# Attention and feed-forward layers in one kernel: products ordered by array shape, TensorE's stream written out, the shifted x sent sooner, the norm's tiles on ScalarE

## What is computed

```python
for i in range(DEPTH):                       # DEPTH = 6
    x = attn_layer(shift_tokens(x), Wqkv[i], q_scale[i], k_scale[i], Wo[i]) + x
    x = ffn_layer(shift_tokens(x), ln_g[i], ln_b[i], W1[i], b1[i], W2[i], b2[i]) + x
# shift_tokens: the second half of the features comes from the token before
# attn_layer: 16 heads of 64; q, k = l2norm(...) * scale, rotated; softmax(8 q k^T) over
#   the own window of 32 tokens and the one before; times v; times Wo
# ffn_layer: (x - mean) / sqrt(var + 1e-5) * g + b; a * gelu(gate) @ W2 + b2, hidden size 341
```

## Time and profile before

| | |
|---|---|
| median of three runs | 4655.95 us |
| profiled execution, its span | 4656.79 us, 4655.0 us |
| TensorE: matmuls, weight loads | 4112.3 us (88%), 2362.1 us (51%) |
| VectorE, ScalarE, GpSimd | 3561.9 (77%), 2988.6 (64%), 2212.4 us (48%) |
| mean granted clock of TensorE | 0.935 of full speed |
| stretch of the layers | from about 340 to 3780 us of the span |

### The profile page before, as it was taken

How to read it: one execution, slowest core, us unless ns; L and a number is a source line. 1 busy time by engine, 2 the same in 40 slices (tenths; PEclk the granted TensorE clock), 3 DMA queues, 4 the chain that set the end, 5 groups by cost and what they waited for, 6 DMA issues and landing times. The chain is left out here.

```text
span 4655.0 us, 112822 instructions
## 1 busy us (share of the span) xinstructions
PE 4112.3 (88%) x40172; PEld 2362.1 (51%) x40175; DVE 3561.9 (77%) x8496; ACT 2988.6 (64%) x5496; POOL 2212.4 (48%) x1392
## 2 busy tenths in 40 slices
PE   8969999999999999999999999999999953747635
PEld 5644555555555555555555555555555532635533
DVE  7878888888888888888888888888888846356441
ACT  3427777777777777777777777777777745645302
POOL 0006665665656656566566656656565500140006
PEclk9989999999999999999999999999999975868557
DMA  1013222322223222232222322223222200000202
GB/s 41 1 54 67 62 58 62 80 59 61 60 60 81 63 59 60 58 82 65 59 59 60 76 65 63 57 64 75 64 60 61 58 17 12 1 1 6 82 9 35
DMA packets 187828, 246.44 MB, mean 53 GB/s; under 512 B 88677, under 2 KB 129383, under 8 KB 187367
## 3 DMA queue, kind: packets, MB, share of 16 engines
q1 hardware_dynamic: 182054, 240.47, 22.2%
q0 software_dynamic: 5632, 4.33, 0.7%
HBM read 41.65 MB, written 14.30 MB: 12 GB/s over the span
## 5 line engine op out<-in xcount | busy, mean ns | idle before, releaser
L1234 POOL TENSOR_TENSOR f_rot_a<-f_rot_a,f_norm 128x1024 f32<-128x1024 f32 x384 | 730.4, 1902 | 996.1 <-DVE f_norm L1073 963.6
L1226 POOL TENSOR_TENSOR f_rot_a<-f_rot_a,f_rot_b 128x1024 f32<-128x1024 f32 x384 | 908.5, 2366 | 246.3 <-issue 213.6
L832 PE MATMUL f_bank<-f_w_vo,f_xs_t 128*64 128x512 f32 x3072 | 828.5, 617 | 24.5 <-ACT f_vo L1303 24.5
L1303 ACT ACTIVATE f_vo<-f_bank 128x512 f32<-128x512 f32 x768 | 457.0, 595 | 395.9 <-PE f_bank L832 385.9
L1294 ACT ACTIVATE f_squares<-f_bank 128x512 f32<-128x512 f32 x768 | 456.4, 594 | 295.5 <-PE f_bank L819 215.6
L1052 DVE TENSOR_TENSOR f_rot_a<-f_bank,f_rot 128x512 f32<-128x512 f32 x768 | 525.0, 684 | 83.4 <-DVE f_stat L1101 42.3
L1055 DVE TENSOR_TENSOR f_rot_b<-f_bank,f_rot 128x512 f32<-128x512 f32 x768 | 516.8, 673 | 0.0
L864 PEld LDWEIGHTS f_bank<-f_k_t,f_q_t 128*32 128x32 f32 x12288 | 313.6, 109 | 315.4 <-issue 162.4
L1059 DVE TENSOR_REDUCE f_sums<-f_squares 128x16 f32<-128x1024 f32 x384 | 464.9, 1211 | 1.6
L1315 ACT ACTIVATE f_k_t<-f_bank 64x512 f32<-64x512 f32 x768 | 449.2, 585 | 4.8 <-PE f_bank L854 0.3
L1240 POOL TENSOR_TENSOR f_prob<-f_score,f_stat 128x512 f32<-128x512 f32 x384 | 400.4, 1043 | 98.6 <-DVE f_stat L1105 98.6
(11 more groups left out here) (445 smaller groups left out, 7235.4 us busy)
## 6 DMA issues: line engine op xcount, KB each, us to landing
f_vo_off<-f_vo SPq DMA_DIRECT2D x1152, 128.0 KB, 2.3
f_vo_off<-f_vo SPq DMA_DIRECT2D x384, 64.0 KB, 2.0
f_w_qk<-in_Wqk SPq DMA_DIRECT2D x12, 512.0 KB, 5.9
f_vo_dram<-f_vo_pair SPq DMA_DIRECT2D x48, 128.0 KB, 1.8
f_x_shifted<-s_all SPq DMA_DIRECT2D x48, 128.0 KB
f_x_shifted<-s_all SPq DMA_DIRECT2D x48, 127.0 KB
f_w_vo<-f_vo_dram SPq DMA_DIRECT2D x10, 512.0 KB, 4.0
e_w<-in_e_W SPq DMA_DIRECT2D x2, 2048.0 KB, 12.1
```

The lines of the kernel that those rows point to most:

```text
L832: done = nc.tensor.matmul(bank[V][64 * n:64 * n + 64, :], x, w_vo[:, 4 * g:4 * g + 4, n, :], start=True, stop=True)
L1226: nc.gpsimd.tensor_tensor(rot_a[:, slot, :, :], rot_a[:, slot, :, :], rot_b[:, g, :, :], ALU.add).then_inc(rot_summed, 1)
L1234: nc.gpsimd.tensor_tensor(heads, heads, over(norm[:, 16 * g:16 * g + 16], [128, 16, HEAD_DIM]), ALU.mult).then_inc(qk_normed, 1)
L1303: nc.scalar.activation(vo[:, g, 2 * (t % 2) + j, :], flat(V), ACT.Copy).then_inc((va_copied, vb_copied)[j], 1)
```

## The change

The order of the products in TensorE's body changes so that the value products, the scores and the mix stand in two blocks of four a step; a value product is cut into four parts of 32 columns instead of two of 64. TensorE's loop over passes 3 to 47 is written out; the class `Steady` makes these passes take the loop's branches. The bodies of the other engines are put into an order that goes with it: on VectorE both rotations of k stand together, `total` and `invert` of group 1 always come a step later, `highest` comes after the rotations of q; on ScalarE `exponential` of group 1 always stands ahead of `copy_q`, and the value copies and the other exponential move; on GpSimd `weigh` goes ahead of `scale`. `shift_x` is issued ahead of `shift_values(p, r - 1, 1)` in the third step. The feed-forward norm's four tiles go from VectorE (`normalise`, subtract and multiply) to ScalarE (scale and offset), in two halves in the second step, and VectorE makes the offset, -mean x inverse root, for all four tiles in one small operation.

```diff
@@ -469,6 +469,16 @@
+class Steady(int):
...
+  def __add__(self, n):
+    return Steady(int(self) + n)
...
+  def __sub__(self, n):
+    return Steady(int(self) - n)
...
 def shifted_layers(nc, x_all, ident, ident_bf, dram):
@@ -584,11 +595,11 @@
-      return not isinstance(p, int) or 0 <= p * PASS_TILES + t < LAST * PASS_TILES
+      return not isinstance(p, int) or isinstance(p, Steady) or 0 <= p * PASS_TILES + t < LAST * PASS_TILES
...
-      return not isinstance(p, int) or 0 <= p - back < LAST
+      return not isinstance(p, int) or isinstance(p, Steady) or 0 <= p - back < LAST
@@ -708,6 +719,9 @@
             shift_values(p, r - 1, 0)
+          if r == 2 and (q > 0 or not first):
+            shift_x(p - 1, (q - 1) % PASSES)
+          if r > 0 or q > 0 or not first:
             shift_values(p, r - 1, 1)
@@ -728,8 +742,6 @@
               load_pair(p + 1)
-          if r == 2 and (q > 0 or not first):
-            shift_x(p - 1, (q - 1) % PASSES)
           if q == 0 and r == 2 and not first:
...
               good_for_layer(w_vo_in[g], layer)
@@ -828,8 +840,9 @@
         x = chunk_x(t)[:, 64 * j:64 * j + 64]
-        for n in range(2):
-          done = nc.tensor.matmul(bank[V][64 * n:64 * n + 64, :], x, w_vo[:, 4 * g:4 * g + 4, n, :], start=True, stop=True)
+        for w in range(4):
+          at = 32 * (w % 2)
+          done = nc.tensor.matmul(bank[V][32 * w:32 * w + 32, :], x[:, at:at + 32], w_vo[:, 4 * g:4 * g + 4, w // 2, :], start=True, stop=True)
         return done
       def values_a(p, t, g):
@@ -962,7 +975,6 @@
           if on(r - 1):
-            values_a(p, r - 1, 1)
             turn_q(p, r - 1, 0)
...
             turn_prob(p, r - 2, 0)
@@ -970,7 +982,6 @@
             turn_k(p, r - 1, 0)
-            values_b(p, r - 1, 1)
           if on(r):
...
           if r == 0 and has(p, 0):
@@ -979,8 +990,15 @@
             up_proj(p - 2, 0)
...
           if on(r - 1):
+            values_a(p, r - 1, 1)
             scores(p, r - 1, 0)
+          if on(r - 2):
+            mix(p, r - 2, 0)
+          if on(r - 1):
+            values_b(p, r - 1, 1)
...
             turn_q(p, r - 1, 1)
...
             project_q(p, r, 1)
@@ -997,18 +1015,18 @@
             up_proj(p - 2, 1)
-          if on(r - 2):
-            mix(p, r - 2, 0)
...
           if on(r):
             values_a(p, r, 0)
+          if on(r - 2):
+            mix(p, r - 2, 1)
           if on(r - 1):
...
             values_b(p, r, 0)
-          if on(r - 2):
-            mix(p, r - 2, 1)
...
-      stream(pe, body)
...
+      for p in range(LAST + 3):
+        body(Steady(p) if 3 <= p < LAST else p)
...
     def _(dve):
@@ -1120,18 +1138,15 @@
-      def normalise(p):
+      def offsets(p):
...
         if live(p + 2, 0):
...
         if has(p, 1):
-          dve.wait_ge(f_turned, p)
-        for t in range(PASS_TILES):
-          last = nc.vector.tensor_scalar(f_n[:, 128 * t:128 * t + 128], x_shifted[:, t, :], f_mv[:, t, 0:1], norm[:, 32 + t:33 + t], ALU.subtract, ALU.mult)
-          if t < PASS_TILES - 1:
-            chain.mark(last)
-        last.then_inc(f_normed, 1)
+          dve.wait_ge(f_normed, p + 1)
+        nc.vector.scalar_tensor_tensor(f_offset[:, :], f_mv[:, :, 0], -1.0, norm[:, 32:32 + PASS_TILES], ALU.mult, ALU.mult).then_inc(f_measured, 1)
...
         n = FF[k][1]
@@ -1153,45 +1168,43 @@
             rotate(p, r, 0, 1, 0)
-          if r < 3 and on(r - 2):
-            invert(1)
-          if on(r):
             rotate(p, r, 0, 1, 1)
-          if r == 3 and on(r - 2):
+          if on(r - 2):
             total(p, r - 2, 1)
...
           if r == 1 and has(p, 2):
-            normalise(p - 2)
+            offsets(p - 2)
           if on(r - 3):
...
             length(p, r, 0)
-            rotate(p, r, 1, 1, 0)
           if on(r - 1):
             highest(p, r - 1, 0)
+          if on(r):
+            rotate(p, r, 1, 1, 0)
           if r == 1 and has(p, 3):
...
             rotate(p, r, 1, 1, 1)
+          if on(r - 1):
+            total(p, r - 1, 0)
+            invert(0)
           if on(r):
...
             inverse_lengths(p, r)
-          if on(r - 1):
-            total(p, r - 1, 0)
-            invert(0)
           if r == 3 and has(p, 2):
             hide(p - 2, 1)
-          if on(r - 1):
-            highest(p, r - 1, 1)
           if on(r):
...
             rotate(p, r, 1, 0, 1)
+          if on(r - 1):
+            highest(p, r - 1, 1)
           if r == 0 and has(p, 2) and not on(r):
...
             chain.mark(inverse_roots(32, 32 + PASS_TILES))
@@ -1199,8 +1212,6 @@
             aggregate()
-          if r != 2 and on(r - 1):
-            total(p, r - 1, 1)
         chain.reset()
       stream(dve, body)
@@ -1254,10 +1265,10 @@
             add_up(p, r, 0)
-            scale(p, r, 0)
           if on(r - 1):
...
           if on(r):
+            scale(p, r, 0)
             add_up(p, r, 1)
       stream(pool, body)
@@ -1335,6 +1346,15 @@
+      def normalise(p, half):
+        act.wait_ge(f_measured, p + 1)
+        if half == 0 and has(p, 1):
+          act.wait_ge(f_turned, p)
+        for t in (2 * half, 2 * half + 1):
+          last = nc.scalar.activation(f_n[:, 128 * t:128 * t + 128], x_shifted[:, t, :], ACT.Identity, bias=f_offset[:, t:t + 1], scale=norm[:, 32 + t:33 + t])
+        if half == 1:
+          last.then_inc(f_normed, 1)
...
       def affine(p):
...
         act.wait_ge(f_turned, p + 1)
@@ -1363,37 +1383,39 @@
             shift_in(0, p + 1)
-          if r < 3 and on(r - 2):
+          if on(r - 2):
             exponential(p, r - 2, 1)
           if on(r - 1):
-            copy_values(p, r - 1, 1, 0)
             copy_q(p, r - 1, 0)
-          if r == 3 and on(r - 2):
-            exponential(p, r - 2, 1)
           if on(r - 2):
...
             square(p, r, 0, 0)
+          if r == 1 and has(p, 2):
+            normalise(p - 2, 0)
           if on(r - 1):
...
             seed(p, r - 1, 0)
-            copy_values(p, r - 1, 1, 1)
           if on(r):
             square(p, r, 1, 1)
+          if r == 1 and has(p, 2):
+            normalise(p - 2, 1)
           if r == 0 and has(p, 0):
...
           if on(r - 1):
+            copy_values(p, r - 1, 1, 0)
+            exponential(p, r - 1, 0)
+            seed(p, r - 1, 1)
+            copy_values(p, r - 1, 1, 1)
             copy_q(p, r - 1, 1)
...
             square(p, r, 1, 0)
-          if on(r - 1):
-            exponential(p, r - 1, 0)
-            copy_k(p, r - 1, 1)
-            seed(p, r - 1, 1)
           if on(r - 2):
             copy_prob(p, r - 2, 1)
+          if on(r - 1):
+            copy_k(p, r - 1, 1)
           if on(r):
...
           if r == 0 and has(p, 0):
```

More of the change, by code:

```diff
@@ L533, in shifted_layers @@
         f_mv = sb("f_mv", [128, PASS_TILES, 2])
+        f_offset = sb("f_offset", [128, PASS_TILES])
         f_n = sb("f_n", [128, PASS_TOK])
@@ L575, in shifted_layers @@
         f_gate, gate_in, f_gelu, f_up = sem("f_gate"), sem("gate_in"), sem("f_gelu"), sem("f_up")
-        f_hidden, f_done, x_stored = sem("f_hidden"), sem("f_done"), sem("x_stored")
+        f_hidden, f_done, x_stored, f_measured = sem("f_hidden"), sem("f_done"), sem("x_stored"), sem("f_measured")
         ctx.callback(clear, nc, used)
```

## The result

The changed kernel takes 4727.2 us (median of 4 runs, 4720.9 to 4732.4) against 4655.7 (4 runs): 1.015 times the time before, interval 1.0135 to 1.017. It is 71 us slower where I predicted 20 us faster, and outside my range of 4515 to 4715. The profiled execution took 4724.9, its span is 4723.1.

What follows compares the result with a forecast made beforehand. TensorE's stream was taken as the bound: a pass of 70.7 us less 2.3 (old waits) and 4.7 (shapes), plus 6.6 (new waits), gives 70.3; over 48 passes -20, so 4656 becomes 4636 us, range 4515 to 4715.

Steps and rivals of the forecast that it cites:

- What bounds the kernel: Whole loop: the pass goes at the pace of TensorE's stream; only shortening it or making it wait counts.
- The shapes: TensorE's products: fewer changes of array width, saving 1.18 us a step, 4.7 a pass.
- TK0: Transposes of k, head group 0: wait for ScalarE's copy of q, 2.4 us in the fourth step.
- TK1: Transposes of k, head group 1: wait in every step, 0.25 to 0.6 us, behind ScalarE's copies.
- The chains: Copies that TensorE's products wait for in the new order: 6.6 us of added waits a pass.
- the scores of the second step: Second step, head group 0: scores wait from 7.7 to 8.8 us, 1.1, behind ScalarE's norm tiles.
- the pause at TK0 of the fourth step: Fourth step, TensorE: waits of 0.6 and 2.4 us, before the transposes of q and of k.
- TQ0: Transposes of q, head group 0, fourth step: a wait of 0.6 us for GpSimd's `scale`.
- rival (c): Pause in the fourth step halves TensorE's clock: up to 3.4 us a fall, 4690 to 4800 us; chance 0.20.
- the first step: First step of a pass: 15.8 us by the prediction's terms, including a 0.6 us wait at TK1.
- The stream written out: TensorE's loop over passes: removing its branch gains 0 to 0.2 us a pass; 0 taken.
- The table load: ScalarE, fourth step: load of 1.28 us without the skill page's extra drain, which would make the time 4703.

Runs made afterwards that it cites:

- e12: Kernel of e9 with the shifted x sent ahead of the second group's value shifts: 4593.3 us.
- e7: Changed kernel with the norm's four tiles back on VectorE: 4722.5 us.
- e6: Kernel before, looped and in its old order, with the value products in four blocks of 32 columns: 4782.8 us.
- e9: Kernel before in its old order, with value products in four blocks of 32 columns and TensorE's stream written out: 4589.5 us.
- e2: Changed kernel with eight extra products of the identity filling TensorE's pause in the fourth step: 4661.7 us.
- e4: Changed kernel with VectorE's stream written out too: 4691.1 us.
- e1: Changed kernel with ScalarE's copy of q ahead of the exponential in the fourth step: 4634.6 us.
- e5: Kernel before with TensorE's stream written out and nothing else: 4653.5 us.
- e11: Changed kernel with TensorE's stream in a loop again: 4862.2 us.
- e8: Changed kernel with e1 and e4 together, and ScalarE's copy of q for group 1 ahead of the seed and the value copy: 4597.5 us.
- e3: Changed kernel with the value products back to two blocks of 64 columns: 4720.9 us.

## Why the prediction was wrong

**What bounds the kernel** was right: every gain and loss above lies in TensorE's stream or its waits. Taking 134.8 us of waits from VectorE (e12), or four tiles a pass (e7), changed nothing that can be measured.

**The shapes** were priced right by block: 0.88 between narrow products, 3.60 a block as laid out. The third step shows the whole saving: 16.75 less the waits of TK0 (0.21) and TK1 (0.24) is 16.30, against 17.41 in which TensorE had no listed wait, 1.11 saved where 1.18 was predicted. The part that the narrow value blocks have in it shows by itself in e6 and e9: 0.44 and 0.55 in the second and third steps.

**The chains** on ScalarE were right to 0.2 us. TK0 came at 5.94 behind PK0, against 5.96, the scores of the second step at 8.65, against 8.8, and TK1 4.76 behind S0, against 4.97. That last difference halves TK1's waits: 0.24 a step (0.20 in the second), 0.9 a pass, where the sum has 1.75. Without falls the steps are 16.86, 18.04, 16.75 and 18.9, against 15.8, 18.4, 17.0 and 19.15. Together they are 70.6, near the 70.3 predicted, and that nearness is luck: three steps came out 0.25 to 0.36 better than laid out, and the first 1.06 worse.

**The step that failed first: what follows the pause at TK0 of the fourth step.** I had split it into 0.6 ahead of TQ0 and 2.4 ahead of TK0. In the trace TQ0 doesn't wait, and the whole stands in one piece of 2.85. I had a row for exactly this, a fall after 2.8 us without a matmul, and one for 2.4 without a fall. I put my 2.4 to 3.1 beside both and gave the falls 0.20. With the pause between two rows of opposite outcome, 0.20 had no ground, and the sum itself carried the clock at nothing; the sum of 0.6 and 2.4 alone pointed to the upper row. The price of a fall was wrong the other way. I took 3.4 us, from 6.8 at half clock, while 30 of the 36 last 3.4 and cost 1.65 in the median; the six of 6.8 cost 2.9. So rival (c) is what happened: it takes 1.4 of the 1.97 us between the pass predicted and the pass measured. The Trainium skill's page "TensorE: Matmul & The Clock Gate", section "Why this matters for your kernels", says that idle gaps give the clock back; 35 falls behind 43 pauses of 2.85 and none behind the pauses of 1.07 in e2 agree.

**The second term that was missing: the first step**, 16.86 against 15.8. My lay-out let VectorE run through its loop end. The 0.93 us was there to be read in the old trace, and I passed over it since TensorE didn't wait for it there. In the new order the rotation for PK1 stands right behind it. Writing VectorE out gives back 0.81 (e4), 36 us; the other 0.25 stays, with a wait of 0.28 of the fold for the gate still in e4's first step.

**The third: where a layer begins.** 2.7 us at each of five changes in e1, most of it a wait for the weights' DMA, 0.3 a pass in the mean. I had looked at passes inside a layer alone.

The sum: 70.3 predicted, +1.4 for the falls, +1.06 for the first step, -0.36, -0.25 and -0.25 for the other three, +0.3 for the layers gives 72.2, and 72.27 was measured.

**The stream written out** was priced right at 0 for the kernel as it stands (e5), and read wrong in its meaning. I took it for a small saving of a branch; it is what lets the 32-column blocks pay. Without it they cost 135 us in the new order (e11) and turn 66 us of gain into 127 of loss in the old one (e6 against e9).

**The table load.** The exponential started 1.30 after its load (655.49 to 656.79), with no drain behind it, as in the earlier trace rows.

**What was expected of the change as a whole** came from another place: the narrow value blocks alone, with the stream written out, gain 66 us (e9). The new order, as it stands, adds waits and falls of the clock worth more than the switches of shape that it removes; with three of them mended it comes to 4597 (e8), level with the old order at best. Its steady pass is 68.8 then, against e9's 69.3, so it could win if the loss at the layer changes were mended as well. That wasn't tried.

## What to carry to other kernels

Lay out a pause as one piece, from the last matmul to the next, and look for the nearest pauses in the trace on both sides of it: what matters is whether the clock fell behind them, and if the new pause lies between them, neither outcome can be taken as the likely one. A reordering that moves an operation next to a loop's end inherits that end's idle time, even if nothing waited for it before. When a loop body grows, compare the instruction queue's packets: a body that is fetched again shows itself there and as "issue" at the loop's first product.

## What was unexpected of the hardware

- TensorE's clock went from 1.00 to 0.50 (from the 2.4 GHz level to the 1.2 GHz level) behind 35 of 43 pauses of 2.85 us, mostly for 3.40 us, behind 4 of 43 pauses of 2.54 us (e3), and behind three pauses of 1.95 to 2.04 us where a layer begins (one in the changed kernel, two in e1). The length alone doesn't decide: eight pauses of the same 2.85 had no fall, and I can't say from these traces what told them apart. Adding 1.95 us of useless products a pass made the kernel 66 us faster.
- A loop body of TensorE with each value product in four blocks in place of two, 108 KB in place of 100, is fetched again in each pass: 457 packets of instructions for 59, and 3.4 us of standstill a pass. Written out in full, the stream of 48 passes takes 352 packets and shows no such standstill.
- VectorE stands 0.93 us at its loop's end in each pass, before and after, under the name of whatever it waited for last; written out, 0.30 is left in the same place (e4).
